# A chain of attention and feed-forward blocks on one core: the last attention's scores in three fp16 passes, and ahead of values and output product in TensorE's order

## The reference

```python
# x: layer-normed (8, 256, 512); h_ctx_kv: (8, 256, 512); T = 256 context tokens
q = (x @ wq).reshape(B, L, 16, 128);  k, v = (x @ wk), (x @ wv)        # 4 key/value heads of 128
k_ctx, v_ctx = (h_ctx_kv @ wk_ctx), (h_ctx_kv @ wv_ctx)
q, k, k_ctx = rms_norm(q, q_norm_w), rms_norm(k, k_norm_w), rms_norm(k_ctx, k_norm_w)
q = q * cos + rotate_half(q) * sin;  k = k * cos + rotate_half(k) * sin
k_full, v_full = concat([k_ctx, k]), concat([v_ctx, v])                # 512 keys, causal on the last 256
scores = einsum('blhd,bmhd->bhlm', q, k_full) / sqrt(128) + mask
out = einsum('bhlm,bmhd->blhd', softmax(scores), v_full)
return out.reshape(B, L, 2048) @ wo
```

## Time and profile before

| | |
|---|---|
| median of 3 runs | 3557.46 us (3552.07 to 3559.20) |
| profiled execution, its own time | 3551.15 us |
| its span in the trace | 3549.4 us |
| stage 6, from the first to the last scores | 2201.2 to 3278.6 us |
| busy over the span | PE 83%, DVE 73%, ACT 46%, POOL 25% |
| stretch 2500 to 2550 us | PE 45.68, DVE 37.41, ACT 24.02, POOL 12.37 us busy |

### The profile page before, as it was taken

The page is one execution under the profiler, slowest core; times in us unless marked ns, Lnnn a source line. Parts: engine busy times, 40 slices in busy tenths (PEclk is TensorE's granted clock), DMA queues, the critical chain, the costliest instruction groups (busy, mean ns, idle before and its releaser), DMA issues.

```text
span 3549.4 us, 50395 instructions
## 1 busy us (share of the span) xinstructions
PE 2950.5 (83%) x18610; PEld 1731.0 (49%) x18610; DVE 2605.0 (73%) x4530; ACT 1642.6 (46%) x2565; POOL 880.2 (25%) x1293
## 2 busy tenths in 40 slices
PE   3899898885668888668878866999999999998998
PEld 1343476663334444246656633444444444444665
DVE  4799869999856666488888877777777777776333
ACT  3000044444335555219877884444444444455343
POOL 2454200000000000005656676222222222221000
PEclk8899999997879999889998978999999999999999
DMA  7222022212210110210000021000000000011000
GB/s 262 88 80 77 28 60 66 61 54 71 50 30 22 25 31 10 92 36 2 1 1 1 1 89 57 7 7 7 1 7 7 1 7 1 7 40 59 13 18 18
DMA packets 52642, 132.51 MB, mean 37 GB/s; under 512 B 6416, under 2 KB 19536, under 8 KB 51152
## 3 DMA queue, kind: packets, MB, share of 16 engines
q1 hardware_dynamic: 43216, 96.11, 8.9%
q10 hardware_dynamic: 9216, 33.56, 3.1%
HBM read 119.03 MB, written 4.19 MB: 35 GB/s over the span
## 4 chain that ended last, share of the span: by engine, by line
PE 36%; DVE 18%; issue 10%; ACT 6%; POOL 1%; DMA 0%; DVEq 0%; SPq 0%; POOLq 0%; ACTq 0%
PE psum L1093 11%; PE psum L2437 4%; PE psum L1913 3%; PE psum L2478 3%; ACT area_g L2003 2%; PE psum L2462 2%; DVE area_c L2056 2%; PE psum L1927 2%; PE psum L1315 2%; PE psum L1334 2%; PE psum L2447 2%; DVE area_a L1651 2%; PE psum L1294 1%; DVE small L2726 1%; PE psum L1948 1%
## 5 line engine op out<-in xcount | busy, mean ns | idle before, releaser
L2003 ACT ACTIVATE area_g<-area_a 128x2048 bf16<-128x2048 f32 x156 | 310.7, 1996 | 47.2 <-DVE area_a L2074 30.2
L1913 PE MATMUL psum<-area_c,ident_bf 128*128 128x128 bf16 x3584 | 243.1, 231 | 102.6 <-DVE area_c L2056 102.5
L172 POOL TENSOR_TENSOR rstd<-mean_var,eps_col 128x2 f32<-128x2 f32 x65 | 16.6, 256 | 1140.2 <-DVE mean_var L581 527.0
L2726 DVE TENSOR_REDUCE small<-psum 128x1 f32<-128x384 f32 (+1 forms) x256 | 158.9, 621 | 184.5 <-PE psum L2438 184.4
L515 PE MATMUL psum<-area_b,area_g 128*128 128x512 f32 x640 | 279.9, 597 | 16.0 <-DVE area_g L464 8.0
L1913 PEld LDWEIGHTS psum<-area_c,ident_bf 128*128 128x128 bf16 x3584 | 225.6, 104 | 132.1 <-DVE area_c L2056 125.5
L2437 PE MATMUL psum<-area_b,stage 128*128 128x512 f32 (+1 forms) x512 | 237.3, 546 | 0.0
L659 PE MATMUL psum<-xT_high,area_a 128*128 128x256 f16 x1024 | 235.6, 279 | 1.4 <-DVE xT_low L596 1.4
L659 PE MATMUL psum<-xT_low,area_a 128*128 128x256 f16 x1024 | 235.2, 279 | 0.0
L2596 ACT ACTIVATE area_g<-psum 128x384 f16<-128x384 f32 (+1 forms) x256 | 139.4, 545 | 169.4 <-PE psum L2447 167.5
L515 PEld LDWEIGHTS psum<-area_b,area_g 128*128 128x128 f32 x640 | 120.8, 191 | 174.4 <-issue 158.4
(11 more groups left out here) (407 smaller groups left out, 7539.8 us busy)
## 6 DMA issues: line engine op xcount, KB each, us to landing
stage<-in_w ACTq DMA_DIRECT2D x24, 512.0 KB, 4.4
stage<-in_w SPq DMA_DIRECT2D x24, 512.0 KB, 3.7
area_g<-in_toeplitz SPq DMA_DIRECT2D x32, 256.0 KB, 3.4
area_b<-in_ctxT SPq DMA_DIRECT2D x15, 512.0 KB, 3.9
area_b<-area_b SPq DMA_DIRECT2D x24, 256.0 KB, 3.7
stage<-in_ctxT SPq DMA_DIRECT2D x9, 512.0 KB, 3.9
x_stream<-in_x SPq DMA_DIRECT2D x4, 1024.0 KB, 8.8
area_c<-in_ctxT SPq DMA_DIRECT2D x4, 1024.0 KB, 15.5
```

The costliest lines, as they stand in the source:

```text
L1913: last = nc.tensor.matmul(psum[:, 1, t_ * P:(t_ + 1) * P], identb[:, :], above5[:, t_, c * P:(c + 1) * P], start=(c == 0), stop=(c == KE - 1))
L2003: nc.scalar.activation(junk5[t_], z5[b % 3][:, t_, :], ACT.Sign, bias=fine5[:, par, t_:t_ + 1], scale=-1.0, accum_out=signs5[:, t_:t_ + 1] ...
L2726: nc.vector.tensor_reduce(nmax6[:, n % 2:n % 2 + 1], psum[:, 2 + n % 2, 0:nk], AX.X, ALU.min).then_inc(sig("nmax6_ready"), 1)
```

## The change

The diff changes four things in stage 6.

1. Queries and keys are held as a high and a low fp16 part in the same bytes. ACT writes the high part (`query_out` now in fp16, and a new `key_high`), DVE the low part (a new `query_low` in every unit, and `key_out` is now a subtraction of the high part from PSUM). `scores` becomes three fp16 matmuls: high by high, high by low, low by high. Bank 7 is free for `project_q` once `query_low` is done.
2. In PE's loop `values(u - 1)` and `project_out(u - 1, 0)` move from ahead of `scores(n + 1)` to behind it.
3. `tables6` works out two scales, so that the fp16 parts are in range, with eight more linked DVE instructions, and scales three tables where it scaled one.
4. In the entry to the stage ACT's order of `key_high`, `query_in`, `key_in` and `output_high` changes, and `query_low(0)` is put ahead of `key_out(0, 4)` on DVE. `exps` and `normalise` stay on ACT and DVE.

Some semaphores are merged (`x4_added` with `x6_added`, `hid7_ready` with `hid_ready`), with offsets on the waits and no other effect on the order.

```diff
@@ tables6
+            dc.link(nc.vector.scalar_tensor_tensor(out=abs_w6, in0=norm_w6, scalar=-1.0, in1=norm_w6, op0=ALU.mult, op1=ALU.max))
+            dc.link(nc.vector.tensor_reduce(top6w, abs_w6, AX.X, ALU.max))
+            dc.link(nc.vector.tensor_scalar(top6w, top6w, ROW_TOP, 1e-12, ALU.mult, ALU.max))
+            dc.step(nc.vector.reciprocal(S1("rq6"), top6w[:, 0:1]))
...
-            dc.step(nc.vector.tensor_scalar(rope6[:, 0], rope6[:, 0], -SC6, None, ALU.mult))
+            for tab, r, c in ((rope6[:, 0], "rq6", -1.0), (rope6[:, 1], "rk6", SC6), (key_w6[:, :], "rk6", SC6)):
+                dc.step(nc.vector.tensor_scalar(tab, tab, S1(r), c, ALU.mult, ALU.mult))
@@ scores
-                nc.tensor.matmul(psum[:, 2 + n % 2, 0:nk], qT6[:, u % 2, h, :], kT6[:, b % 2, 0:nk // P, g, :], start=True, stop=False)
+                for qp, kp in ((0, 0), (0, 1), (1, 0)):
+                    nc.tensor.matmul(psum[:, 2 + n % 2, 0:nk], qT6[:, u % 2, qp, h, :], kT6[:, b % 2, 0:nk // P, kp, g, :],
+                                     start=(qp + kp == 0), stop=False)
@@ pe_stage6, the loop
-                if h == 0:
-                    if u:
-                        values(u - 1)
                 if h == 1:
-                    if u:
-                        project_out(u - 1, 0)
                     if b + 1 < B and w % 2:
                         turn_k(b + 1, w - 1)
...
                 if n + 1 < 4 * UNITS:
                     scores(n + 1)
+                if h == 1 and u:
+                    project_out(u - 1, 0)
+                if h == 0 and u:
+                    values(u - 1)
                 turn_p(n)
@@ act_stage6
-                nc.scalar.activation(qT6[:, u % 2], psum[:, 7, :].rearrange("p (h q) -> p h q", h=4), ACT.Copy).then_inc(sig("qT6_ready"), 1)
+                nc.scalar.activation(qT6[:, u % 2, 0], psum[:, 7, :].rearrange("p (h q) -> p h q", h=4),
+                                     ACT.Copy).then_inc(sig("qT6_high_ready"), 1)
...
+                if h == 1 and w % 2 and b + 1 < B:
+                    key_high(b + 1, w - 1)
@@ dve_stage6
-                dve.wait_ge(sig("kT6_ps_ready"), 4 * b + j // 2 + 1)
-                nc.vector.tensor_copy(kT6[:, b % 2, key_block(j)], psum[:, kv_bank(b, j), :].rearrange("p (g n) -> p g n", g=G3)).then_inc(sig("kT6_ready"), 1)
+                dve.wait_ge(sig("kT6_high_ready"), 4 * b + j // 2 + 1)
+                nc.vector.tensor_tensor(kT6[:, b % 2, key_block(j), 1], psum[:, kv_bank(b, j), :].rearrange("p (g n) -> p g n", g=G3),
+                                        kT6[:, b % 2, key_block(j), 0], ALU.subtract).then_inc(sig("kT6_ready"), 1)
...
+            def query_low(u):
+                dve.wait_ge(sig("qT6_high_ready"), u + 1)
+                nc.vector.tensor_tensor(qT6[:, u % 2, 1], psum[:, 7, :].rearrange("p (h q) -> p h q", h=4), qT6[:, u % 2, 0],
+                                        ALU.subtract).then_inc(sig("qT6_ready"), 1)
...
+                if h == 2 and u + 1 < UNITS:
+                    query_low(u + 1)
                 turned_low(n)
```

More of the change, by code:

```diff
@@ L2224, in build @@
         oT6 = stage[:, 0, 512:1024].bitcast(F16).rearrange("p (v h q) -> p v h q", v=2, h=4)
[L2225 removed]
+        qT6 = stage[:, 1, :].bitcast(F16).rearrange("p (a v h q) -> p a v h q", a=2, v=2, h=4)
         first_ctx6 = stage[:, 1, :].rearrange("p (k s) -> p k s", k=KD)
@@ L2574, in query_out, with key_high @@
                     act.wait_ge(sig("ctx_part_low_ready"), B + TT)
-                nc.scalar.activation(qT6[:, u % 2], psum[:, 7, :].rearrange("p (h q) -> p h q", h=4), ACT.Copy).then_inc(sig("qT6_ready"), 1)
+                nc.scalar.activation(qT6[:, u % 2, 0], psum[:, 7, :].rearrange("p (h q) -> p h q", h=4),
+                                     ACT.Copy).then_inc(sig("qT6_high_ready"), 1)
+            def key_high(b, j):
+                act.wait_ge(sig("kT6_ps_ready"), 4 * b + j // 2 + 1)
+                nc.scalar.activation(kT6[:, b % 2, key_block(j), 0], psum[:, kv_bank(b, j), :].rearrange("p (g n) -> p g n", g=G3),
+                                     ACT.Copy).then_inc(sig("kT6_high_ready"), 1)
             def x_high(b, t_):
@@ L2617, in act_stage6 @@
             value_in(0, 3)
+            key_high(0, 0)
             query_in(0)
+            key_high(0, 2)
             key_in(0, 4)
@@ L2623, in act_stage6 @@
             value_in(0, 7)
-            for n in range(4):
-                output_high(n)
+            key_high(0, 4)
+            output_high(0)
+            output_high(1)
+            key_high(0, 6)
+            output_high(2)
+            output_high(3)
             query_in(1)
@@ L2790, in dve_stage6 @@
             key_begin(0, 6)
+            query_low(0)
             key_out(0, 4)
```

40 lines of the change are left out of this document (24 added, 16 removed).

## The result

| | before | changed |
|---|---|---|
| median | 3558.3 us (3552.1 to 3559.7, 4 runs) | 3526.7 us (3522.9 to 3532.5, 4 runs) |
| ratio | | 0.9916, 95% interval 0.9896 to 0.9936 |
| profiled execution: own time, span | 3551.15, 3549.4 us | 3523.6, 3521.7 us |

The account below looks back on a forecast made before the run. PE was taken to set the pace, 83% busy, with DVE three quarters full beside it. Seven sequences -48, the last -4 and the entry +3 made -49 us: 3508 us from a median of 3557.46, range 3475 to 3532.

Parts of the forecast that it names:

- The passes' work: Scores on PE: three fp16 passes save 0.16 or 0.21 us a score, 47 us in all, 5.9 a sequence.
- the walk: Stage 6 units stepped through `turn_p` by `turn_p`: a sequence gains 6.9 us, seven sequences 48 us.
- `values` still starts at 1.21, when ACT is ready: Unit w=2, h=0: `values` keeps its start 1.21 us after `turn_p`, so the next `turn_p` comes 0.70 us earlier.
- I count nothing: Bank 7 freed later by `query_low`, before `project_q`: no cost counted, at most 0.2 us a unit.
- The entry: Start of stage 6: added DVE instructions (scales, scalings, `query_low(0)`) count in full, +3 us, between 1 and 5.
- ACT's entry is later by up to 3 us, but DVE takes its results later still: Entry to stage 6: ACT's delay of up to 3 us adds nothing to the +3 us counted for DVE.
- The last sequence: Eighth sequence, no key work, ACT sign passes in four units: half a microsecond gained per unit, 4 us.
- DVE takes the order's gain back: Rival, units: `query_low` or `key_high` late in the h=0 to h=2 chain; gain 12 to 35 us, about 3532; chance 0.17.
- The passes save nothing: Rival, scores: 384 columns as slow as 512, DVE takes back the rest; within 7 us; chance 0.02.
- PE's waits vanish: Rival, units: they come near PE's own work; gain 65 to 120 us, about 3470; chance 0.12.
- DVE becomes the pace: Rival, units: `normalise` ends every step, passes give nothing, `query_low` and `key_high` lie on the path; 3612 us; chance 0.04.
- each pass pays its load: Rival, scores: every fp16 pass pays its 0.10 us weight load; +31 us, with the entry 3591 us; chance 0.01.

Follow-up runs that it names:

- order-only run: The kernel before with only TensorE's new order (scores ahead of values and output product), fp32 scores in one pass: 3526.76 us, ratio 0.9916.
- `query_low(0)` early: Changed kernel with the entry's first low-query subtraction moved on DVE to right behind the second key copy-out, `key_out(0, 2)`: 3525.17 us, ratio 0.9909.
- `key_end` later: Changed kernel with DVE's end of a key chunk moved from ahead of an odd unit's first `normalise` to right behind it: 3526.96 us, ratio 0.9919.
- three other profiles with the same code there: Changed kernel with `query_low(0)` early, with `key_end` later, and with a reordered entry; last sequence 105.3, 106.3 and 106.1 us.

## Why the prediction was right in sign and a third too large

**The passes' work: right.** The score of 384 keys in w=2 takes three passes of 0.163 us (timeline, PE, changed kernel; L2453 is the mask):

```profile
2505.73 0.65 PE L2451 MATMUL psum<-area_b,stage 128*128 128x384 f16 x3
2506.22 0.22 PE L2453 MATMUL psum<-tri,ident_bf 128*128 128x128 bf16 x1
```

Summed over a steady sequence from start to start, the scores without the mask take 18.2 us for 24.1 (7.8 for 10.35 with 384 keys, 10.4 for 13.75 with 512), 5.9 us less, as forecast. Columns count (0.163 us for 384, 0.216 for 512) and the loads don't. The Trainium skill's rule that loads overlap only for other row groups ("TensorE: Matmul & The Clock Gate", Part 3, "The mechanism") is again not what the trace shows. The same section of the Trainium skill also lets a load be pulled ahead when it targets the background weight buffer, and that fits. The failure is what these 5.9 us are worth: 1.7, by the order-only run.

**The units: the walk was right in shape, 1.25 us a sequence too good.** Forecast 14.7, 16.8 and 16.5 for w=2, 3 and 6; measured 14.99, 16.90, 16.56. The gains of w0 to w7 were 0.54, 0.48, 0.41, 0.54, 0.86, 0.85, 1.22 and 0.75 us, 5.65 for 6.9. (Over seven sequences 41.3 for 48, since the first one gained 7.5.) `turn_p` of h=1 starts at 6.13 in w=2, where DVE's side gave 6.05. Two sentences failed. The first is "`values` still starts at 1.21, when ACT is ready": they start at 1.36. ACT, changed kernel and before (L2582 and L2568 the start of `query_in`, L2616 and L2596 `turned`):

```profile
2510.69 0.69 ACT L2582 ACTIVATE area_g<-psum,scalars 128x512 f32<-128x512 f32 x1 [2.83 <-PE psum L1093]
2511.28 0.68 ACT L2583 ACTIVATE area_g<-psum,scalars 128x512 f32<-128x512 f32 x1
2511.85 0.49 ACT L2616 ACTIVATE area_g<-psum 128x384 f16<-128x384 f32 x1
```

```profile
2511.43 0.69 ACT L2568 ACTIVATE area_g<-psum,scalars 128x512 f32<-128x512 f32 x1 [2.83 <-PE psum L1093]
2512.02 0.68 ACT L2569 ACTIVATE area_g<-psum,scalars 128x512 f32<-128x512 f32 x1
2512.59 0.49 ACT L2596 ACTIVATE area_g<-psum 128x384 f16<-128x384 f32 x1
```

ACT works without a gap from the end of `project_q`, which lies ahead of the scores, to `turned`. So `values` hang on the end of `project_q` and not on `turn_p`, and what the passes save between `project_q` and `turn_p`, 0.16 us, is a wait in front of `values`. The second is "I count nothing" for bank 7: `project_q` starts 0.13 us late for `query_low`, the 0.13 of the run without it. With the two, 0.7 becomes 0.41, what was measured; by the steps, 0.08 us of the shortfall lie at h=1 (6.13 for 6.05), 0.04 at h=2 and 0.14 at h=3. The term that failed is thus the 0.16 us for each of the scores at h=2 and h=3: the walk took both in full, and in w=2 the two together earn nothing. The order's part, 0.36 forecast, came to 0.40. The signs came much as told: in the steady sequence `values` wait 0.32 to 0.37 us where 0.2 was forecast, and `turn_p` at h=1 waits 0.17 to 0.58 for 0.6.

**The entry: +3 us forecast, +7.4 to the first score and +8.9 to the first `values`.** The tables' part was right (6.34 us for 3.79, +2.55). The step that failed is "ACT's entry is later by up to 3 us, but DVE takes its results later still": DVE waits 2.10 us for ACT's `query_in(0)`, behind projections at half clock and the new `key_high(0, 0)`. (Item 4 of "The change" has ACT's order of `query_in`, `key_in` and `output_high` changing; in the diff these keep their order, and the four `key_high` are put among them.) Nor did the sum ask which PE instruction waits for `query_low(0)` and what stands behind it: that is most of the remaining 2.7 us. From `query_begin(0)` to the first score the changed kernel takes 29.5 us, with `query_low(0)` early 28.0, without it 26.9, before 26.8. `key_end` later, with the changed kernel's entry, takes 28.7, so 0.8 us of this is scatter. In the first unit `project_q(2)` waits 2.53 us for `query_low(1)` behind a low part of the output weights, 1.5 us more there.

**The last sequence: -4 forecast, +0.7 measured** (-0.4 to -1.4 in the three other profiles with the same code there). The units were given half a microsecond of gain each. PE's waits of `values` did fall, from 8.4 us to 4.9 (they stand behind a sign); but those of `turn_p` for `normalise` rose from 5.0 to 9.9, and PE's clock fell, from a mean of 1.00 to 0.95 (changed kernel; L2915 is a sign, L2616 `turned`):

```profile
3180.26 1.05 ACT L2915 ACTIVATE area_a<-area_a 128x1024 f16<-128x1024 f32 x1
3181.21 0.49 ACT L2616 ACTIVATE area_g<-psum 128x384 f16<-128x384 f32 x1
```

```profile
3173.58 0.90 PE L2462 MATMUL psum<-ident,xn 128*128 128x128 f32 x3 [0.17 <-DVE xn L2767]
```

That `turn_p` lasts 0.90 us for 0.50, at the lower level. The stretch 3150 to 3200, changed kernel and order only:

```profile
3150.00:3200.00 50.00, 39.69 (x200) 20.01 (x199) 32.15 (x73) 30.70 (x60) 8.58 (x10) 0.93 0.41 119
```

```profile
3150.00:3200.00 50.00, 41.18 (x201) 20.76 (x200) 31.72 (x73) 31.22 (x66) 8.35 (x9) 1.00 0.46 139
```

Together 5.9 of the missing 17.3 us are the entry, 6.7 the units and 4.7 the last sequence.

**What was luck.** That 3526.7 us lies inside the range is in part luck. Half of the change, three passes and the 47 us of PE work that they save, brought nothing in total (3526.76 us without them), and the range holds the result only because it took in the upper half of a rival.

**The rivals.** "DVE takes the order's gain back" (about 3532) came nearest in time (it gave 12 to 35 us of gain), but not by its mechanism, in which the order's gain was lost and the passes' kept; it was the other way round. "The passes save nothing" was given 0.02, for slow columns. Its conclusion came true through the entry, the waits and the clock. "PE's waits vanish", "DVE becomes the pace" and "each pass pays its load" are out: the waits changed their place, and 5.4 us of DVE work cost 0.26.

**Still open.** What the loop of a unit hangs on, exactly. The steps show two links, the end of `project_q` through ACT to `values`, and DVE's chain to `normalise` at h=1; but every wait taken away (at h=0, at h=1, by less PE work) came back elsewhere within a unit. Of the 5.9 us that scores save in a sequence 1.7 show in its length and 2.4 as listed waits (6.60 for 4.25). The remaining 1.9 are in no listed wait: from start to start, the time behind the mask grows by 0.8 us and that of the product's matmuls by 0.9. No run took a whole link, such as ACT's `query_in` ahead of `turned`, out of the way.

## What to carry to other kernels

Price a saving by the wait that stands behind it, not by its engine's busy share: PE was busy 127.9 of 136.55 us in a steady sequence and three fp16 passes took 5.9 us of work from it, yet 1.7 showed, while pure reordering gave 3.9. When one change holds two ideas, run each alone before believing either. And walk the entry like the steady state: a new instruction that frees a bank is waited for by the producer, and everything queued behind that producer pays.
